# Gather-and-sum stages of a four-layer graph kernel: each one-hot product issued once

## The reference, cut to what matters

```python
def _gcn_layer(x, W, b, src, dst, norm, n_nodes):      # layer one, used twice
    xt = x @ W
    msg = xt[src] * norm[:, None]
    agg = jax.ops.segment_sum(msg, dst, num_segments=n_nodes)
    return jax.nn.relu(agg + b)
...
norm = edge_weight * jax.lax.rsqrt(deg_out[src] * deg_in[dst] + EPS)
...
# layer four
scaled = (X @ W + b) * dinv[:, None]
msg = jax.ops.segment_sum(scaled[col], row, num_segments=N)
out = (msg + scaled) * dinv[:, None]
...
x = _layernorm(x + _L0_gnn_ref(...), axis=-1)
x = _layernorm(x + _L1_gnn_ref(...), axis=-1)
x = _layernorm(x + _L2_gnn_ref(...), axis=-1)
x = _layernorm(x + _L3_gnn_ref(src, dst, x, ...), axis=-1)
```

## Time and profile before

| what | us |
|---|---|
| median of 3 runs | 10826.19 (10809.07 to 10837.02) |
| span of the profiled execution, first to last instruction | 10786.8 |
| TensorE matmul busy | 6660.1 (62%) |
| VectorE busy | 5888.6 (55%) |
| GpSimd busy | 5638.7 (52%) |
| ScalarE busy | 2865.5 (27%) |
| stage one, gathers issued | 3188.0 to 4407.1 |
| stage two, gathers issued | 4473.4 to 5670.1 |
| stage four, gathers issued | 9493.2 to 10709.5 |

### The profile page before, as it was taken

The page is one execution under the profiler, slowest core; times in us unless marked ns, Lnnn a source line. Parts: engine busy times, 40 slices in busy tenths (PEclk is TensorE's granted clock), DMA queues, the critical chain, the costliest instruction groups (busy, mean ns, idle before and its releaser), DMA issues. The chain is left out here.

```text
span 10786.8 us, 111774 instructions
## 1 busy us (share of the span) xinstructions
PE 6660.1 (62%) x26173; PEld 4039.9 (37%) x26173; DVE 5888.6 (55%) x17189; ACT 2865.5 (27%) x9329; POOL 5638.7 (52%) x5879
## 2 busy tenths in 40 slices
PE   2201344437867777677776777775555589767775
PEld 1101233334435555555554111133333334345554
DVE  8915533430026666544445999976566579932223
ACT  0000001006852222100002888862222246500000
POOL 5776566661016666466661777734555510056664
PEclk9999855558989989899997999996656679989998
DMA  2000111104553333333333777744666645423333
GB/s 78 6 6 5 35 46 44 48 27 142 175 186 90 91 90 90 107 88 90 88 88 68 213 214 213 214 116 140 185 187 185 192 127 176 139 85 90 90 90 77
DMA packets 796235, 1193.07 MB, mean 111 GB/s; under 512 B 161213, under 2 KB 631923, under 8 KB 788941
## 3 DMA queue, kind: packets, MB, share of 16 engines
q0 software_dynamic: 259712, 606.96, 21.5%
q1 hardware_dynamic: 535885, 578.95, 16.6%
HBM read 926.73 MB, written 258.64 MB: 110 GB/s over the span
## 5 line engine op out<-in xcount | busy, mean ns | idle before, releaser
L1161 POOL DMA_INDIRECT ring<-scaled_table,idx_s x832 | 786.7, 946 | 1202.0 <-DVEq L193 771.4
L1029 POOL DMA_INDIRECT big<-x_table,rec_d_sb x808 | 799.7, 990 | 1137.2 <-DMA x_table<-big 716.8
L1439 PE MATMUL bank<-ring,wts 128*128 128x512 f32 x1664 | 934.4, 645 | 396.2 <-DVE acc L1426 181.5
L1760 POOL DMA_INDIRECT ring<-att_table,rec_d_sb x808 | 776.2, 961 | 747.5 <-DVE acc L1870 284.3
L1122 PE MATMUL bank<-big,acc 128*128 128x256 f32 x3232 | 894.7, 425 | 374.2 <-issue 344.4
L1196 PE MATMUL bank<-ring,acc 128*128 128x256 f32 x3232 | 873.1, 417 | 359.8 <-issue 329.7
L1365 POOL DMA_INDIRECT ring<-y_table,idx_s x832 | 803.0, 965 | 466.7 <-DVEq L193 188.2
L334 POOL DMA_INDIRECT rec_s<-acc,big x784 | 840.5, 1072 | 376.0 <-issue 253.2
L1161 POOL DMA_INDIRECT ring<-h_table,rec_d_sb x808 | 764.4, 946 | 498.6 <-PEq L1198 236.5
L334 POOL DMA_INDIRECT rec_d<-x_res,big x784 | 750.6, 957 | 500.7 <-DVE big L597 252.5
L1122 PEld LDWEIGHTS bank<-big,acc 128*128 128x128 f32 x3232 | 643.2, 210 | 625.4 <-issue 541.2
(11 more groups left out here) (352 smaller groups left out, 13729.6 us busy)
## 6 DMA issues: line engine op xcount, KB each, us to landing
weights_dram<-acc SPq DMA_DIRECT2D x104, 1024.0 KB, 4.5
ring<-weights_dram SPq DMA_DIRECT2D x832, 128.0 KB
rows_spill<-ring SPq DMA_DIRECT2D x808, 128.0 KB
big<-rows_spill SPq DMA_DIRECT2D x808, 128.0 KB, 2.2
ring<-key_dram SPq DMA_DIRECT2D x49, 1024.0 KB
big<-dl_dram SPq DMA_DIRECT2D x50, 512.0 KB
ring<-y_table,idx_s POOLq DMA_INDIRECT x832
ring<-scaled_table,idx_s POOLq DMA_INDIRECT x832
```

Of the source, the lines that this page charges most:

```text
L1029: g.indirect_dma_start(out=xg[:, c % RG, :], out_offset=None, in_=x_table, in_offset=bass.IndirectOffsetOnAxis(ap=recd3i[:, c, D_IDX:D_IDX ...
L1161: g.indirect_dma_start(out=slot[:, c % ring_len, :], out_offset=None, in_=table, in_offset=bass.IndirectOffsetOnAxis(ap=index(c), axis=0)) ...
L1439: pe.matmul(ps[6 + u % 2], oh1[c // 4 % 2][:, c % 4, :], mid[:, c % 2, 0:512], start=(c % GS == 0), stop=(c % GS == GS - 1)).then_inc(summ ...
L1760: g.indirect_dma_start(out=ag[:, n % R3, :], out_offset=None, in_=att_table, in_offset=bass.IndirectOffsetOnAxis(ap=recd3i[:, n, D_IDX:D_I ...
```

## The change

In stages one and two the loop that issued the product twice is gone, and the product is issued once. In stage four the four matmul calls are one call per chunk, which starts the accumulation at the even chunk and stops it at the odd one. Nothing else differs: rings, waits, signals and the other engines' programs are the same.

```diff
@@ first_tensor
-                for _ in range(2):
-                    pe.matmul(half_bank(c), onehot[:, c % 16, :], xg[:, c % RG, 0:D], start=True, stop=True)
+                pe.matmul(half_bank(c), onehot[:, c % 16, :], xg[:, c % RG, 0:D], start=True, stop=True)
                 if c % 2 == 1:
                     pe.drain().then_inc(summed.s, 1)
@@ second_tensor
-                for _ in range(2):
-                    pe.matmul(half_bank(c), hot20[:, c % 20, :], hg[:, c % R2, :], start=True, stop=True)
+                pe.matmul(half_bank(c), hot20[:, c % 20, :], hg[:, c % R2, :], start=True, stop=True)
                 if c % 2 == 1:
                     pe.drain().then_inc(summed.s, 1)
@@ fourth_tensor
-                if c % 2 == 0:
-                    pe.matmul(ps[u % 8][:, 0:D], oh20[:, c % 20, :], sg[:, c % R4, :], start=True, stop=True)
-                    pe.matmul(ps[u % 8][:, 0:D], oh20[:, c % 20, :], sg[:, c % R4, :], start=True, stop=False)
-                else:
-                    pe.matmul(ps[u % 8][:, 0:D], oh20[:, c % 20, :], sg[:, c % R4, :], start=False, stop=True)
-                    pe.matmul(ps[u % 8][:, D:2 * D], oh20[:, c % 20, :], sg[:, c % R4, :], start=True, stop=True)
+                pe.matmul(ps[u % 8][:, 0:D], oh20[:, c % 20, :], sg[:, c % R4, :],
+                          start=(c % 2 == 0), stop=(c % 2 == 1))
                 if c % 2 == 1:
                     pe.drain().then_inc(summed.s, 1)
```

## The result

| kernel | median us (runs) | ratio to before, 95% interval | span of the profiled execution |
|---|---|---|---|
| before | 10817.63 (10786.97 to 10837.02, 4) | | 10786.8 |
| after | 10728.92 (10677.85 to 10738.03, 4) | 0.9912 [0.9885, 0.9939] | 10726.9 |

What follows compares the result with a forecast made beforehand. TensorE was taken to set the pace, with GpSimd waiting on a full ring until a pair is summed. Closer gathers (283 us) plus shorter stage ends (17 us) made 300 us off, giving 10526 us; range 10240 to 10880.

Steps and rivals of the forecast that it cites:

- The loop between TensorE and GpSimd as the bound: Three stages: GpSimd waits for TensorE's drains; at its own 1.25 us a gather they would shrink by 577 us.
- The price of the pair: TensorE's loop per pair of chunks falls from 2.19 to 1.33 us at full clock, 3.98 to 2.26 at the lower.
- The clock: TensorE's mean granted clock in the three stages falls from 0.90 to between 0.5 and 0.75, at no cost counted.
- the cover: GpSimd's 2.50 us a pair hides TensorE's 2.26 us; without it the lower clock costs up to 0.93 us a pair.
- The accumulation in stage four and VectorE: Stage four sums over two matmul groups instead of four, priced at nothing; VectorE's work stays and does not take over.
- The holds: Drains that end late in the three stages: a gather would cost 1.37 us, holds included, saving 283 us.
- rival B: Three stages: gather traffic itself sets 2.97 us a pair, removed work becomes longer holds; 0 to -20 us, 10815 us; chance 0.13.
- The prediction's own signs: Three stages: gathers 1.31 to 1.43 us apart, drain waits under 350 us, most pairs 2.50 us apart, clock under 0.9.
- The tails: Pairs summed after each of the three stages' last gather run faster; 17 us saved in all.
- A: Three stages: GpSimd bounds fully at 1.25 us a gather, holds following matmul count or shrinking into slack; 10226 us; chance 0.18.
- C: Three stages: lower clock with unchanged holds, fewer than 6.4 pairs between holds, 1.527 us a gather; +101 us, 10927 us; chance 0.16.
- D: Stages one and two: duplicate products are already dropped, so the change does nothing; excluded because 3229 matmuls each were counted.

Runs made afterwards that it cites:

- g3: The kernel after, unchanged, run in a set without holds: ratio 0.9991 [0.9970, 1.0011] to the kernel before.
- e3: The kernel before with three products a chunk instead of two in stages one and two, in a set without holds: 9418.13 us, ratio 1.0475.
- f2: The kernel after, unchanged, run again in a second set with holds: 10650.83 us, ratio 0.9892 to the kernel before.
- m1: The kernel after, each pair's drain in the three stages replaced by an increment on its last matmul, with holds: 10650.67 us, ratio 0.9881.
- m2: The kernel after with half of each row gathered in stages two and four, in a set with holds: 10659.58 us, ratio 0.9890.
- h3: The kernel before with three products a chunk instead of two in stages one and two, in a set without holds: ratio 1.0458.
- k2: The kernel before with three products a chunk in stages one and two, run once more in a set without holds: ratio 1.0481.
- e1: The kernel after, each pair's drain in the three stages replaced by an increment on its last matmul, without holds: 8988.08 us, ratio 1.0006.

## Why the prediction was wrong, step by step

**The loop between TensorE and GpSimd as the bound: right where there are holds, and only there.** Gathers start 1.25 us apart in stages two and four as soon as no hold is in the way (g3), so the prize of 1.25 us was read rightly for these. For stage one it was not quite: 1.309 us there is the floor.

**The price of the pair: right.** 1.33 and 2.26 us a pair were forecast, 1.33 and 2.27 are in the rows after. A product at 0.43 us is confirmed by e3: 404 pairs longer by 0.54 us (3.04 instead of GpSimd's 2.50).

**The clock: right in size, its price open where there are holds.** 0.5 to 0.75 was forecast, and it is 0.67, 0.68 and 0.66 in the three stages. Without holds it costs nothing, as was said: in g3 the program's clock falls to 0.78, and the ratio is 0.9991 [0.9970, 1.0011]. With holds the cover is partly gone, for which the prediction had named up to 0.93 us a pair and then counted nothing. At full clock TensorE would have saved 0.86 us on each pair, 347 us in stages one and two and 358 in stage four; its busy time fell by 251, 231 and 208. The rest, a quarter to two fifths, went to pairs at the lower level. The Trainium skill's rule in "TensorE: Matmul & The Clock Gate", section "HAM oscillation — how this bites in real kernels", agrees with the trace after in what happens: the pair of 10019.06 runs at full clock (1.10 us), TensorE then idles 3.71 us, and the next pair is at the lower level (2.04 us). That this costs time by itself g3 does not bear out, and g3 is at the lower level without such waits: the longest idle time of TensorE in its stage two, from 40 us after the start on, is 1.8 us, at a granted clock of 0.60.

**The accumulation in stage four and VectorE: right**, nothing shows; VectorE's busy time is the same.

**The holds: this step failed.** It took 1.37 us a gather, "the middle between 1.25 and 1.42". Measured were 1.453, 1.431 and 1.428, which gives 807 x 0.057 + 807 x 0.052 + 831 x 0.036 = 117 us instead of 283. The reason given was that "a hold is made good sooner, and more of it falls into time in which GpSimd goes on". Both halves are borne out: GpSimd waited 664 us for 702 us of holds before, and waits 476 us for 1258 us of holds after. What failed is what stands behind them without a reason, that there would be no more hold time to make good than before. It grew by four fifths. Stage by stage the account closes within 3 us: TensorE's busy time fell by 251, 231 and 208 us, the holds grew by 200, 184 and 171, which leaves 50, 47 and 37, and the stages are 48, 47 and 36 us shorter. The account shows where the time went; why less work makes more hold time it does not show. More gathers now follow one another without a gap (89% in stage two, 78% before), which goes along with it. This is the mechanism of rival B ("what is taken away turns into longer holds"), not to the full: B said 0 to -20 us, and it was -132. It had been given 0.13.

The prediction had 1.42 us, from the start of stage four, as the bad end of the term's range, and the stages came out at 1.43 to 1.45, beyond it. With 1.42 as the value the sum would have been 807 x 0.091 + 807 x 0.063 + 831 x 0.044 = 161 us, 1.5% of the time. But that this row comes close is partly luck: the same count of 30 gathers at the start of stage two, also before, gives 1.35 us (4473.4 to 4513.98), and the gathers up to the first stop in stages two and four of the kernel after give 1.36 and 1.32. It was no bound either, as it was read from 30 gathers.

The prediction's own signs say the same. "The forecast is wrong if the holds per gather do not shrink": they grew, from 0.29 to 0.51 us. The waits for the drain fell to 476 us and not under 350. Most pairs were to start 2.50 us apart, in step with GpSimd; in the kernel after at most 1% of them start 2.4 to 2.6 us apart, where in stage two of g3, without holds, it is half.

**The tails: right.** 17 us were forecast, and from the last gather to the end of the stage it is 2.0 + 5.5 + 7.0 = 14.5 us less. 117 + 14 is the 131 us of the windows.

**The time.** The three stages were forecast at -300 us and gave -132. The forecast further said that no other stage would move by over 30 us: the output stage moved by 61, with the clock and not with the change. Its 61 us are seen in the profiled execution (10728.81 us); the other three took 10738.03, 10729.04 and 10677.85, and their stages are not on record, so the median may hold them too. In f2, whose profiled execution does not have them, the ratio is 0.9892 [0.9854, 0.9930], not apart from 0.9912 [0.9885, 0.9939]. The 10728.92 us lie in the range of 10240 to 10880, on the side of its slow end. The 39.4 us that the prediction put on top of the span are no fixed distance: each run on record whose span is known takes 1.8 to 2.0 us more than it. They are scatter between executions, so the forecast joined the median of one set of executions to the span of another.

**Rivals.** A (10226 us) is refuted: the holds neither follow the number of matmuls nor shrink into the slack. C (slower) is refuted by its sign: the clock fell, but the gathers came closer. It needed a clock near 0.5 throughout and holds of unchanged length, and had neither; its limit of 6.4 pairs between holds took the long cycle of the earlier trace rows for the usual one. D was excluded, and the halved counts bear that out.

**What stays open.** What makes a hold, and why their sum grows as TensorE's work shrinks. Shown is that it is not the drain instruction (m1) and not the bytes of the gathers (m2), and, in the one hold that was followed, that no data is missing. No run with holds changed the number of gathers; m2 has 32 packets for each gather of stage two instead of 48, and its holds are the same, so a third fewer packets do not shrink them either. A rival that nobody tested is the recording of the executions itself. The traces with holds have 67,370 to 78,164 records of semaphore updates, the fourteen without 158,821 to 159,063. In stage two it is 5801 records before, 3717 after and 14302 in g3; in the stage behind the attention logits, which lasts 681 to 684 us everywhere, it is 16033 in all of them. So records are missing where holds are, and more of them in the kernel after than before. They are missing too in layer two's message stage (14,561 of 31,705 in the kernel after), which is no slower. Whether the recording delays TensorE's signals, or both have one cause, is not shown, as every execution on record has its span and clock from a recording. Whether it takes a certain pace of gathers was to be seen from three products where there are holds; h3 and k2 ran where there are none, so this is not known. Nor is what the three stages would take with holds and the full clock. Why whole sets of runs are free of holds isn't known either.

## What to carry over

When a wait in the trace lasts longer than the work that it waits for, price the work and the wait apart: taking away work gives back only its share, and the wait may grow into the space. Sum such a wait over the whole stage before pricing it: one cycle picked from the timeline (seven pairs here) and one count of 30 gathers (1.42 us here, 1.35 a stage earlier) are samples, not bounds. And before a gain of one per cent is believed or given up, see whether it is there in another set of runs: this one is 0.99 in one kind and 1.00 in the other.

## What the hardware did that was not expected

- One program, two times. The kernel after takes 10727 us of span in one set and 8981 in another (g3). From barrier to barrier, the sorting stage is 3143 against 2182 us, stages one, two and four 1247, 1186 and 1258 against 1127, 1033 and 1111, and the stage of the attention logits 1351 against 1047. Layer two's message stage, whose gathers start 1.57 us apart in both, is the same (1321 and 1322), and so are the stages without gathers, but for the output stage.
- In the sorting stage the difference is not in TensorE's holds alone: GpSimd stands idle for 721.3 us between its last indirect DMA there (2470) and the first gather of stage one in the kernel after with holds, and for 55.3 us in e1. TensorE computes the edge weights meanwhile (matmuls of L771 and L797, 2460 to 3138); in g3 these run from 1339 to 2031, beside the indirect DMAs. So a step that overlaps them where there are no holds comes behind them where there are. The delay is there before them: the 49 batches of the sort that end with a copy by ScalarE (L401) run from 826 to 1304 in g3 and from 1229 to 2407 in the kernel after. What they wait for was not followed.
- A stage in which TensorE is busy without a break can stay at the lower clock from its start to its end (189.7 us for 128.6). It did so in six of the twenty profiled executions, with one product as with two; what decides it is not known.
